# The last FFN group's layers 2 to 4, placed between the first quads' projections of a gated delta-rule layer

## The reference, cut to what matters

```
xn  = layernorm(x)                       # (16, 256, 128)
# attention branch, on a second norm of xn (with affine): the gated delta rule, token by token
S = a_t * S;  S += b_t * kn (v_t - kn S);  o  = q_t S
R = aR_t * R; R += g_t * kn (clip(v_t - pred) - kn R);  o += q_t R
attn = o @ Wo.T + xn
# FFN branch, hidden width 512
h = silu(xn @ w1 * s1) * (xn @ w2 * s2)  # layer 1
h = gelu(h @ h1 * sh1)                   # layer 2
h = gelu(h @ h2 * sh2)                   # layer 3
ffn = h @ w3 * s3                        # layer 4
out = x + attn + ffn
```

## Time and profile before

| | |
|---|---|
| median of 3 runs | 2342.6 us (2341.97 to 2350.55) |
| the profiled execution | 2340.59 us, its span 2338.5 us |
| TensorE busy | 97% of the span |
| TensorE weight loads | 82% |
| VectorE, ScalarE, GpSimd busy | 72%, 53%, 51% |
| mean granted clock of TensorE | 0.987 of full speed |

### The profile page before, as it was taken

The page is one execution under the profiler, slowest core; times in us unless marked ns, Lnnn a source line. Parts: engine busy times, 40 slices in busy tenths (PEclk is TensorE's granted clock), DMA queues, the critical chain, the costliest instruction groups (busy, mean ns, idle before and its releaser), DMA issues.

```text
span 2338.5 us, 120262 instructions
## 1 busy us (share of the span) xinstructions
PE 2266.3 (97%) x52544; PEld 1909.1 (82%) x52544; DVE 1692.4 (72%) x3727; ACT 1240.2 (53%) x2391; POOL 1189.3 (51%) x2384
## 2 busy tenths in 40 slices
PE   8999996999999999999999999999999999999997
PEld 3454544898888888988888898898898998888887
DVE  5411017888888788888888888888887888888874
ACT  3333236555555555555555655555565555555540
POOL 0010006666656655666666566666665666666641
PEclk9999997999999999999999999999999999999999
DMA  3000001221112222222112121111212222222221
GB/s 92 0 1 0 21 1 20 42 39 39 37 36 39 46 39 42 39 40 39 38 37 49 38 42 39 37 35 38 39 36 50 39 42 43 44 41 41 42 46 25
DMA packets 306501, 84.92 MB, mean 36 GB/s; under 512 B 280384, under 2 KB 303040, under 8 KB 305984
## 3 DMA queue, kind: packets, MB, share of 16 engines
q1 hardware_dynamic: 304784, 74.89, 16.3%
q10 hardware_dynamic: 1200, 2.36, 0.3%
HBM read 41.53 MB, written 35.65 MB: 33 GB/s over the span
## 4 chain that ended last, share of the span: by engine, by line
PE 91%; DMA 3%; POOL 2%; issue 1%; DVE 1%; SPq 1%; ACT 1%; POOLq 0%; ACTq 0%; DVEq 0%
PE bank L516 12%; PE bank L392 5%; PE bank L539 5%; PE bank L530 5%; PE bank L405 5%; PE bank L496 4%; PE bank L560 3%; PE bank L551 3%; PE bank L478 3%; PE bank L675 3%; PE bank L467 3%; PE bank L616 3%; PE bank L473 3%; PE bank L485 3%; PE bank L458 3%; PE bank L593 3%
## 5 line engine op out<-in xcount | busy, mean ns | idle before, releaser
L1144 POOL TENSOR_TENSOR lane_t<-lane_n,lane_x 128x15 f32<-128x15 f32 (+7 forms) x960 | 318.8, 332 | 371.7 <-DMA lane_n<-n_dram 301.5
L1147 POOL TENSOR_TENSOR lane_x<-lane_x,lane_t 128x15 f32<-128x15 f32 (+7 forms) x960 | 335.6, 350 | 75.2
L516 PE MATMUL bank<-kq,Kt 64*64 64x96 f32 x8192 | 361.5, 232 | 0.6
L516 PEld LDWEIGHTS bank<-kq,Kt 64*64 64x64 f32 x8192 | 315.2, 135 | 3.4 <-issue 3.3
L1343 ACT ACTIVATE oS<-bank 128x512 f32<-128x512 f32 x64 | 38.2, 597 | 351.9 <-PE bank L664 351.9
L1118 POOL TENSOR_TENSOR KQF<-efull,kn 128x768 f32<-128x768 f32 x64 | 124.3, 1942 | 186.4 <-ACT efull L1298 186.4
L1267 ACT ACTIVATE ea<-bank,nba 128x256 f32<-128x256 f32 x256 | 107.5, 471 | 193.1 <-PE bank L478 136.9
L1320 ACT ACTIVATE kend<-Kt,ek 128x64 f32<-128x64 f32 x768 | 189.8, 341 | 0.0
L924 DVE COPY_PREDICATED AS<-cst,bank 128x384 f32<-128x384 int32 x256 | 142.6, 582 | 31.1 <-PE bank L516 28.3
L873 DVE TENSOR_TENSOR_SCAN cum<-rst,dk 128x512 f32<-128x512 f32 x128 | 153.5, 1241 | 0.2
L1129 POOL TENSOR_TENSOR Kt<-ek,kn 128x512 f32<-128x512 f32 x64 | 115.5, 1805 | 71.1 <-ACT ek L1311 71.1
(11 more groups left out here) (158 smaller groups left out, 6338.4 us busy)
## 6 DMA issues: line engine op xcount, KB each, us to landing
XF<-x_dram SPq DMA_DIRECT2D x256, 64.0 KB, 2.3
lane_n<-n_dram SPq DMA_DIRECT2D x128, 124.0 KB, 2.8
x_dram<-lane_x SPq DMA_DIRECT2D x128, 124.0 KB, 2.4
n_dram<-AS SPq DMA_DIRECT2D x256, 32.0 KB, 2.0
n_dram<-AR SPq DMA_DIRECT2D x256, 32.0 KB, 1.7
wt<-in_win SPq DMA_DIRECT2D x4, 640.0 KB, 4.9
out_y<-acc SPq DMA_DIRECT2D x16, 128.0 KB, 2.0
hw<-in_h1T SPq DMA_DIRECT2D x1, 1024.0 KB, 11.7
```

What stands on the lines that cost most here:

```text
L516: ins = pe.matmul(v3(dst[hd[h], o:o + kinds * C], kinds)[:, :, i * SUB:(i + 1) * SUB], Kt[hd[h], m * 96 + i * SUB:m * 96 + i * SUB + C], r ...
L1144: pool.tensor_tensor(tv, lane_n[:, m * SUB + m + 1:m * SUB + BASE].unsqueeze(2).to_broadcast([L, rows, m + 1]), xv[:, m, 0:m + 1].unsqueez ...
L1147: pool.tensor_tensor(xv[:, m + 1:, 0:m + 1], xv[:, m + 1:, 0:m + 1], tv, ALU.subtract).then_inc(s["lane_step"], 1)
```

## The change

FFN's last group (g = 7) stops after its first layer on TensorE and ScalarE. The engines enter attention once the hidden layer of group 7 stands (`h1_sb` = 32), and the rest of the group is issued in slices inside the first bodies: TensorE does slice o of layer 2 after each projection step of quad 0, slice o of layer 3 in the same places of quad 1, and layer 4 after the second product group of quad 0, in banks 4 to 7 and 6. ScalarE's gelus stand behind body(-3) and behind body(-2), VectorE's `add_ffn(7)` behind body(-2). The wait for `ffn_added` = 8 moves: to body(0) on TensorE, VectorE and ScalarE, to body(-1) on GpSimd, since the buffers that FFN still uses are laid over buffers that attention needs only from quads 1, 2 or 3 on. The ones over the first-used buffers (`bsum`, `xnT`, `silu`) are done by then. `squash(1)` comes right after the last silus. The SP queue is not changed.

```diff
...
+            behind = sa("behind", LATE_COLS - (8 * HID + 4 * DM + 9 * FFN_TOK + DM + 16 + 2 * HID + 4 * NBLK))
+            KQF_late = [sbb(f"KQF{i}", 10 * (T - C)) for i in (2, 3)]
+            vt_late = [sbb("vt3", 2 * T)]
+            kendT_late = ringb("kendT", 2, 4 * (T - C))
...
...
             for g in range(GROUPS):
                 first_layer(g)
+                if g == GROUPS - 1:
+                    break
...
-            pe.wait_ge(s["ffn_added"], GROUPS)
+            pe.wait_ge(s["h1_sb"], 4 * GROUPS)
             pe.wait_ge(s["bg_add"], 2)
+            pe.wait_ge(s["down_used"], GROUPS - 1)
+
+            def late_second(o):
+                for k in range(4):
+                    ins = pe.matmul(bank[4 + o][:, :], hw1[:, k * HID + o * P:k * HID + (o + 1) * P], hA[:, k * FFN_TOK:(k + 1) * FFN_TOK], start=(k == 0), stop=(k == 3))
+                ins.then_inc(s["g1_ps"], 1)
+
+            def late_third(o):
+                pe.wait_ge(s["g1_sb"], 4 * GROUPS)
...
+            def late_last(tb):
+                pe.wait_ge(s["g2_sb"], 4 * GROUPS)
...
-            for k in range(-3, LAST + 3):
+            for n, late in ((0, late_second), (1, late_third), (2, None)):
+                if n == 2:
+                    turn_kend(0)
+                project_kq(n)
+                if late:
+                    late(0)
+                project_a(n)
+                if late:
+                    late(1)
+                project_r(n)
+                if late:
+                    late(2)
+                norms(n)
+                if late:
+                    late(3)
+                project_v(n)
+                if n:
+                    for g in range(OPS):
+                        products(n - 1, g)
+                        if n == 1 and g == 1:
+                            for tb in range(4):
+                                late_last(tb)
+            pe.wait_ge(s["ffn_added"], GROUPS)
+            for k in range(0, LAST + 3):
                 body(k)
...
-                add_ffn(g)
-
-            dve.wait_ge(s["ffn_added"], GROUPS)
+                if g < GROUPS - 1:
+                    add_ffn(g)
+
+            dve.wait_ge(s["h1_sb"], 4 * GROUPS)
...
+            body(-3)
+            body(-2)
+            add_ffn(GROUPS - 1)
+            for k in range(-1, LAST + 3):
+                if k == 0:
+                    dve.wait_ge(s["ffn_added"], GROUPS)
                 body(k)
...
+                if g == GROUPS - 1:
+                    squash(1)
+                    break
...
+            body(-3)
+            late_gelus(0)
+            body(-2)
+            late_gelus(1)
+            body(-1)
+            act.wait_ge(s["ffn_added"], GROUPS)
+            for k in range(0, LAST + 3):
                 body(k)
```

More of the change, by code:

```diff
@@ L43 @@
 NCONST = 512
+LATE_COLS = 2 * 10 * (T - C) + 2 * T + 2 * 4 * (T - C) + 2 * NM * C + NM * SUB + 14 * P + 2 * T
 SEMAPHORES = {
@@ L159, in sa @@
                 return pa.enter_context(nc.sbuf_tensor(name, [P, cols], F32))
[L160 to L164, removed]
             hw1 = sa("hw1", 4 * HID)
@@ L167, in delta_rule_layer @@
             w3 = sa("w3", 4 * DM)
-            sc = sa("sc", 16)
-            s3b = sa("s3b", DM)
-            silu = sa("silu", 4 * FFN_TOK)
             hA = sa("hA", 4 * FFN_TOK)
@@ L173, in delta_rule_layer @@
             dn = sa("dn", FFN_TOK)
+            s3b = sa("s3b", DM)
+            sc = sa("sc", 16)
+            w1 = sa("w1", HID)
+            w2 = sa("w2", HID)
+            st = sa("st", 4 * NBLK)
+            behind = sa("behind", LATE_COLS - (8 * HID + 4 * DM + 9 * FFN_TOK + DM + 16 + 2 * HID + 4 * NBLK))
+            bsum = sa("bsum", 16 * NQ)
+            xnT = sa("xnT", B * T)
+            silu = sa("silu", 4 * FFN_TOK)
         with ExitStack() as pb:
@@ L179, in ringb @@
                 return [sbb(f"{name}{i}", cols) for i in range(n)]
+            KQF_late = [sbb(f"KQF{i}", 10 * (T - C)) for i in (2, 3)]
+            vt_late = [sbb("vt3", 2 * T)]
+            kendT_late = ringb("kendT", 2, 4 * (T - C))
+            Zf = ringb("Zf", 2, NM * C)
+            Xc = sbb("Xc", NM * SUB)
+            P1 = Xc
+            Sst = ringb("Sst", 2, P)
+            Rst = ringb("Rst", 2, P)
+            wS = ringb("wS", 2, P)
+            yS = ringb("yS", 2, P)
+            wR = ringb("wR", 2, P)
+            yR = ringb("yR", 2, P)
+            rS = ringb("rS", 2, P)
+            oS = sbb("oS", 2 * T)
+            KQF = ringb("KQF", 2, 10 * (T - C)) + KQF_late
+            vt = ringb("vt", 3, 2 * T) + vt_late
+            kendT = ringb("kendT_first", 1, 4 * (T - C)) + kendT_late
             q = sbb("q", 2 * T)
@@ L194, in delta_rule_layer @@
             kq = sbb("kq", 5 * 2 * T)
-            KQF = ringb("KQF", RING, 5 * 2 * (T - C))
             dec = ringb("dec", RING, NM)
-            vt = ringb("vt", RING, 2 * T)
-            kendT = ringb("kendT", 3, 4 * (T - C))
             lane_n = sbb("lane_n", LANE_W)
             lane_t = sbb("lane_t", 64)
-            Zf = ringb("Zf", 2, NM * C)
             P0 = dk
[L205 to L215, removed]
         n_dram = nc.dram_tensor("n_dram", (2, 4, NM, SUB, SUB), F32).ap()
@@ L441, in _ @@
                 last_layer(g)
-            pe.wait_ge(s["ffn_added"], GROUPS)
+            pe.wait_ge(s["h1_sb"], 4 * GROUPS)
             pe.wait_ge(s["bg_add"], 2)
+            pe.wait_ge(s["down_used"], GROUPS - 1)
[5 more added lines that the diff above has]
+                pe.wait_ge(s["g1_sb"], 4 * GROUPS)
+                for k in range(4):
+                    ins = pe.matmul(bank[4 + o][:, :], hw2[:, k * HID + o * P:k * HID + (o + 1) * P], hB[:, k * FFN_TOK:(k + 1) * FFN_TOK], start=(k == 0), stop=(k == 3))
+                ins.then_inc(s["g2_ps"], 1)
+            def late_last(tb):
+                pe.wait_ge(s["g2_sb"], 4 * GROUPS)
+                for k in range(4):
+                    ins = pe.matmul(bank[6][:, tb * P:(tb + 1) * P], hA[:, k * FFN_TOK + tb * P:k * FFN_TOK + (tb + 1) * P], w3[:, k * DM:(k + 1) * DM], start=(k == 0), stop=(k == 3))
+                if tb == 3:
+                    ins.then_inc(s["down_ps"], 1)
             def xh(n):
@@ L1171, in _ @@
             pool.wait_ge(s["ready"], 1)
-            pool.wait_ge(s["ffn_added"], GROUPS)
+            pool.wait_ge(s["h1_sb"], 4 * GROUPS)
             pool.wait_ge(s["bg_ready"], 1)
             for k in range(-3, LAST + 3):
+                if k == -1:
+                    pool.wait_ge(s["ffn_added"], GROUPS)
                 body(k)
@@ L1234, in _ @@
                     keep_xh(3 * g - 8)
-                elif g >= 6:
-                    squash(g - 6)
+                elif g == 6:
+                    squash(0)
                 if g == 0:
@@ L1243, in _, with late_gelus @@
                     keep_xh(3 * g - 7)
-            act.wait_ge(s["ffn_added"], GROUPS)
+            act.wait_ge(s["h1_sb"], 4 * GROUPS)
             act.wait_ge(s["ready"], 1)
             act.wait_ge(s["nba"], 1)
+            def late_gelus(layer):
+                for o in range(4):
+                    act.wait_ge(s[("g1_ps", "g2_ps")[layer]], 4 * (GROUPS - 1) + o + 1)
+                    act.activation((hB, hA)[layer][:, o * FFN_TOK:(o + 1) * FFN_TOK], bank[4 + o][:, :], ACT.Gelu,
+                                   scale=sc[:, 8 + 4 * layer + o:9 + 4 * layer + o]).then_inc(s[("g1_sb", "g2_sb")[layer]], 1)
             def squares(n):
```

## The result

The changed kernel took 2327.9 us (median of 6 runs, 2325.19 to 2332.81), the kernel before in the same comparison 2342.28 us (6 runs, 2336.84 to 2350.55). The ratio is 0.9939, with an interval of 0.9918 to 0.9959: 14.4 us less, between 9.6 and 19.2. The forecast was 2334.7 (2328 to 2342), no difference beyond 0.5%. The way was right, the size was not: 7.9 us were forecast.

The account below looks back on a forecast made before the run. The fill was taken as one chain through all engines: start 31.4 us earlier, then 18.6, 10.2, 8.9 at the first mask, less 1.0 for clock, leaving 7.9; 2342.6 - 7.9 = 2334.7 us, range 2328 to 2342.

Parts of the forecast that it names:

- the class: Whole kernel's median: within 0.5% of before at chance 0.80, faster by more 0.17, slower by more 0.03.
- Steps 1 and 3: Attention starts 31.4 us earlier; TensorE idles 5.7 us before quad 1's k, first layer 3 slice 2.7 us ahead of need.
- the bounds: Limits on the gain, 3 to 11 us; clock 0.50 until a(1) would end the first layer 3 slice 2.7 us late.
- Steps 2 and 4: Quad 0 with layer 2, quad 1 with layer 3: log decays' table loads 18.6 and 10.2 us earlier, behind each fourth slice.
- Step 5: VectorE before quad 1's kn: add_ffn(7) waits for layer 4, costs about 1.7 us; first mask 8.9 us earlier.
- Step 6: Product groups 3 and 4 after TensorE's 2.8 us idle run at low clock, costing 1.0 us; 7.9 us remain.
- the second hole: TensorE idle 2.8 us from layer 4's end at 363.73 until the first mask is done, near 366.6.
- The reference: Profiled execution of the kernel before, 2340.59 us, whose rows timed each step; runs' median taken 2.0 us above it.
- Rival A: FFN slices fill the fill's idle TensorE time freely: gain up to 23 us, around 2328 us; chance 0.14.
- Rival B: Clock stays at 0.50 from the 5.7 us hole through layer 3: 8.5 us loss, 2351.1 us; chance 0.05.
- Rival C: Mask comes 8 us earlier but something unmoved ends the fill: gain 0 to 3 us, 2341 us; chance 0.12.

Follow-up runs that it names:

- the later comparisons: The unmodified changed kernel run three more times against the kernel before: 2333.36, 2330.49 and 2331.44 us, ratios 0.9948, 0.9951 and 0.9953.
- the shifted add: Changed kernel with VectorE's add of group 7 behind the first four masks instead of ahead of norm_k(1): 2331.42 us, 0.9941 of the kernel before.
- the spread kernel: Changed kernel with the slices spread over three quads, layer 4 and the add in quad 1's products and masks: 2318.87 and 2322.57 us, 0.9901 and 0.9919 of before.
- again: The changed kernel run a second time, nothing altered, against the kernel before: 2333.36 us (8 runs), ratio 0.9948.
- fourth: The changed kernel run a fourth time, nothing altered, against the kernel before: 2331.44 us (12 runs), ratio 0.9953.
- third: The changed kernel run a third time, nothing altered, against the kernel before: 2330.49 us (9 runs), ratio 0.9951.

## Why the prediction was right in its chain and wrong in its size

The measured median lay 0.1 us below the range, and the class was wrong: 0.80 stood on no difference beyond 0.5%. By the later comparisons the gain is 0.47 to 0.52%, at the very edge between the two.

*Steps 1 and 3* held: start 0.06 us behind the hidden product, hole of 5.73 us, a(1) released by the copy of q. The slack of the first layer 3 slice was 0.3 us (0 to 0.7 in the four traces), not 2.7: it ran partly at low clock, as the bounds said, and just made it.

*Steps 2 and 4* held in kind and were too long by 0.7 and 0.5 us. I priced the gates and norms of a quad at 1.13, 1.13 and 1.10 us, as they stand in the earlier trace rows where each follows a wait. Behind a slice they cost 0.86 (317.03 to 317.89 above), only a(1), which still follows a wait, 0.97. That makes 0.8 us for quad 0 and 0.5 for quad 1; the first mask came at 54.7 us behind the hidden product where the sum had 56.05.

*Step 5* held: `add_ffn(7)` stands ahead of kn(1), at 1.7 us, as the shifted add shows. It costs the path nothing to speak of there, since it costs as much wherever VectorE does it ahead of the scaling.

*Step 6* was wrong. It charged 1.0 us for low clock behind the second hole. From first mask to first inverse products the changed kernel took 33.9, 33.7, 34.0 and 34.4 us in four traces, the kernel before 34.2. In the second and third of these traces the clock did drop to 0.50 there. In the second the last four product groups of quad 0 took 5.10 us instead of 3.73, and the span from the mask on was not longer: VectorE was done with the scaling 4.36 us behind the first mask, in the first trace 4.35. So in place of a loss of 1.0 us the runs show 0.2 us less than before (a mean of 34.0 against 34.2).

```profile
365.97 5.10 PE L543 MATMUL bank<-kq,Kt 64*64 64x96 f32 x96 [2.76 <-DVE AS L975]
```

*The reference* was one trace with a fill of 99.15 us; three have a mean of 99.7. So 1.3 of steps 2 to 4, 1.2 of step 6 and 0.5 of the reference are missing from 7.9, which makes 10.9. The 3 us beyond that in the first comparison are scatter. The range should have allowed for that: executions of one kernel differ by 10 to 20 us (2328.89 to 2349.3 in 26 runs of before), and I had taken three runs for the whole of it.

*Rival A* (holes fill freely) fell for this order: k of quad 1 waits 5.73 us. The holes do take work once the slices stand elsewhere, as the spread kernel shows. *Rival B* fell: in all four traces the granted clock was back at 1.00 before a(1), and the fill's mean rose from 0.85 to 0.90. The reading that stands behind B in the prediction, that the first work after each hole is slow, fits the hole of 5.73 us, behind which k stood at 0.50 in all four, and not that of 2.8 us, behind which the clock stayed at 1.00 in two traces and fell a good 1 us later in the other two. *Rival C* fell here, but it is what happened in the variants: a mask 14.4 us earlier gave 5.3, one 1.7 us earlier gave none.

## What to carry to other kernels

Work put into the holes of a pipeline's fill goes behind the link that the other engines wait for, not ahead of it: here the same 31 us of matmuls gave 11 us in one order and about 20 in another by the medians (16 by the fill). A mark moved in the middle of a fill is no gain until the last mark moves; read the trace at both, and read the clock behind the last one before you compare totals. Price a step by how it runs between neighbours, not by a row in which it follows a wait, and take the scatter from more than three runs before naming a class.

## What the runs showed of the hardware

What TensorE's granted clock costs depends on who sets the pace. In the fill, filling the waits with idle matmuls lifted it from 0.85 to 0.98 over 98 us and brought the end of the fill 1.3 to 1.8 us forward. Right behind it, where the recurrence has begun, it costs much more. Two traces of the changed kernel, the first and `again`, from the first to the second inverse products:

```profile
400.30:429.06 28.76, 23.72 (x619) 20.72 (x620) 24.97 (x41) 17.72 (x35) 22.14 (x39) 1.00 0.22 44
```

```profile
398.97:433.02 34.05, 30.40 (x619) 25.67 (x620) 23.42 (x41) 17.66 (x35) 20.42 (x40) 0.75 0.22 42
```

The same work (x619 in the profile) takes 5.3 us longer. The other two traces of this kernel show it too: `fourth` has 28.41 us at 1.00, `third` 34.78 at 0.71. The change doesn't choose between them, and what does is not shown.

So runs of one kernel scatter with the clock: eight runs of the changed kernel lie between 2318.94 us at a mean clock of 0.993 and 2338.28 at 0.987, with 2333.44 at 0.984 among them. Over all 63 runs of the kernel before and 35 of the changed one, a straight line through both gives about 1.5 us less for each 0.001 of mean granted clock, and 3 us of scatter stay around it. That is as large as what was to be measured here, and it is why the traces' marks settled more than the medians did.
